# Scaling an attention layer's output instead of its probabilities, with the value product in another orientation

## The reference

```python
q = (x @ w_q).reshape(b, n, HEADS, DIM_HEAD).transpose(0, 2, 1, 3)
k = (x @ w_k).reshape(b, n, HEADS, DIM_HEAD).transpose(0, 2, 1, 3)
gates = jax.nn.sigmoid((x @ w_gate).reshape(b, n, HEADS, EXPERTS).transpose(0, 2, 1, 3))
sel = jnp.argmax(gates, axis=-1)
gm = jax.nn.one_hot(sel, EXPERTS, dtype=x.dtype) * gates
values = jnp.einsum('bhne,ehdk,bnd->bhnk', gm, value_experts, x)
sim = jnp.einsum('bhid,bhjd->bhij', q * SCALE, k)
...
attn = jax.nn.softmax(sim, axis=-1)
out = jnp.einsum('bhij,bhjk->bhik', attn, values)
out = jnp.einsum('bhne,ehkd,bhnk->bhnd', gm, output_experts, out)
return out.sum(axis=1)
```

## Time and profile before

| | |
|---|---|
| time, median of 3 runs | 2442.16 us (2441.66 to 2443.49) |
| the profiled execution: time, span | 2442.16 us, 2439.8 us |
| TensorE busy | 2118.5 us (87%) |
| VectorE busy | 1668.6 us (68%) |
| ScalarE busy | 883.3 us (36%) |
| GpSimd busy | 616.6 us (25%) |
| mean granted TensorE clock | 0.922 of full |

### The profile page before, as it was taken

How to read it: one execution, slowest core, us unless ns; L and a number is a source line. 1 busy time by engine, 2 the same in 40 slices (tenths; PEclk the granted TensorE clock), 3 DMA queues, 4 the chain that set the end, 5 groups by cost and what they waited for, 6 DMA issues and landing times. The chain is left out here.

```text
span 2439.8 us, 40010 instructions
## 1 busy us (share of the span) xinstructions
PE 2118.5 (87%) x12915; PEld 1156.1 (47%) x12915; DVE 1668.6 (68%) x3418; ACT 883.3 (36%) x1559; POOL 616.6 (25%) x834
## 2 busy tenths in 40 slices
PE   4659999999999789999999899599979999859865
PEld 2634444444444356666666544255544444325431
DVE  4757776786777567777777599477745656436668
ACT  3522212211220056666666444033322222223335
POOL 4641110111111155555555332322100000021201
PEclk8569999999999899999999999699979999979975
DMA  3403212220321321111111000000000000010001
GB/s 100 147 1 71 54 29 59 59 63 17 70 53 42 100 69 36 36 32 32 35 31 35 14 0 1 5 12 12 10 4 0 0 0 0 0 28 13 12 4 34
DMA packets 116410, 80.38 MB, mean 33 GB/s; under 512 B 92777, under 2 KB 111081, under 8 KB 111812
## 3 DMA queue, kind: packets, MB, share of 16 engines
q1 hardware_dynamic: 116292, 78.91, 13.4%
HBM read 55.08 MB, written 2.82 MB: 24 GB/s over the span
## 5 line engine op out<-in xcount | busy, mean ns | idle before, releaser
L1015 PE MATMUL l0f_acc<-l0f_z,w_all 128*128 128x512 f32 x512 | 233.3, 618 | 22.7 <-DVE l0f_z L1227 22.7
L912 POOL TENSOR_TENSOR l0f_v<-l0f_val,l0f_top 64x256 f32<-64x256 f32 x128 | 78.4, 613 | 504.4 <-DVE l0f_val L1190 496.8
L966 PE MATMUL l0f_work<-w_all,l0f_xs 128*128 128x512 f32 x384 | 183.5, 600 | 9.9 <-DVE l0f_val L1185 8.6
L1015 PEld LDWEIGHTS l0f_acc<-l0f_z,w_all 128*128 128x128 f32 x512 | 100.6, 198 | 154.7 <-issue 127.5
L241 POOL TENSOR_SCALAR var_eps<-mean_var 128x4 f32<-128x4 f32 (+1 forms) x64 | 14.7, 229 | 569.5 <-DVE mean_var L225 567.6
L2263 PE MATMUL a_score<-keys_by_head,a_qT 128*64 128x512 f32 x512 | 144.7, 647 | 10.8 <-DMA keys_by_head<-w_all 10.8
L2765 DVE TENSOR_TENSOR l2f_work<-l2f_work,l2f_pu 128x512 f32<-128x512 f32 x104 | 71.5, 688 | 120.5 <-ACT l2f_work L2676 119.0
L2676 ACT ACTIVATE l2f_work<-l2f_pg 128x512 f32<-128x512 f32 x104 | 62.1, 597 | 206.9 <-PE l2f_pc L2616 206.8
L1190 DVE COPY_PREDICATED l0f_val<-l0f_oh,l0f_work 128x512 f32<-128x512 int32 x160 | 116.6, 729 | 22.7 <-PE l0f_work L966 7.8
L2621 PE MATMUL l2f_acc<-l2f_work,w_all 128*128 128x512 f32 x208 | 107.8, 600 | 11.1 <-DVE l2f_work L2769 11.1
L1685 DVE TENSOR_REDUCE l1x_ms_k<-l1x_sq_k 128x8 f32<-128x512 f32 x64 | 43.9, 686 | 102.9 <-ACT l1x_sq_k L1571 102.7
(11 more groups left out here) (369 smaller groups left out, 4873.7 us busy)
## 6 DMA issues: line engine op xcount, KB each, us to landing
l0f_first_mask<-onehots SPq DMA_DIRECT2D x32, 512.0 KB, 5.7
w_all<-onehots SPq DMA_DIRECT2D x32, 512.0 KB, 11.9
l1x_v<-l1x_vr SPq DMA_DIRECT2D x256, 64.0 KB, 2.1
w_all<-in_weights SPq DMA_DIRECT2D x1, 4640.0 KB, 16.6
l0x_m_b<-running_max SPq DMA_DIRECT2D x16, 256.0 KB, 4.5
keys_by_head<-w_all SPq DMA_DIRECT2D x256, 8.0 KB
keys_by_head<-ctxT_all SPq DMA_DIRECT2D x256, 8.0 KB
w_all<-in_weights SPq DMA_DIRECT2D x1, 2500.5 KB, 8.6
```

The lines of the kernel that those rows point to most:

```text
L912: nc.gpsimd.tensor_tensor(v2[a * SEQ:(a + 1) * SEQ, t % 2, b, :, :], val[r, t % 2, :, :].rearrange("p (c a) k -> p c a k", a=2)[:, :, a, : ...
L966: nc.tensor.matmul(value_banks[e % 3][:, :], xs[:, t * P:(t + 1) * P], ve[:, e, :], start=True, stop=True).then_inc(ve_done, 1)
L1015: nc.tensor.matmul(acc[:, :], oe[:, n % E, n // E, :], z[:, n % Z, :], start=(n == 0), stop=(n == C * E - 1)).then_inc(acc_done, 1)
```

## The change

The probabilities are no longer scaled before the value product. They are transposed as soon as the exponentials are there. The value product is turned round: the transposed probabilities are the weights, and `v2`, now with the two heads of a pair side by side and zeros between (cleared once at the start), is the data, so eight matmuls of 128 rows and 128 columns give the output with tokens on partitions. VectorE scales that output from PSUM into a new buffer `og` (`scale_out`); TensorE transposes `og` back, four transposes a tile (`turn_out`), into the bank `turn`, from which ScalarE makes `oT`. The order of the work around it is changed on TensorE, ScalarE and VectorE.

```diff
--- before.py
+++ after.py
@@ -840,12 +840,13 @@
-        v2 = sb("v2", [P, 2, 2, C, HD])
+        v2 = sb("v2", [P, 2, 2, C, 2, HD])
...
+        og = sb("og", [P, H * HD])
@@ -894,6 +894,7 @@
+                nc.gpsimd.memset(v2[:, :, :, :, :, :], 0.0).then_inc(setup_done, 1)
@@ -910,7 +911,7 @@
-                                v2[a * SEQ:(a + 1) * SEQ, t % 2, b, :, :],
+                                v2[a * SEQ:(a + 1) * SEQ, t % 2, b, :, a, :],
@@ -935,7 +936,7 @@
-                pe.wait_ge(setup_done, count(3))
+                pe.wait_ge(setup_done, count(4))
@@ -967,7 +968,7 @@
                         if e == 2 and between:
                             between()
-                        if e == 5 and later:
+                        if e == 4 and later:
                             later()
@@ -984,8 +985,8 @@
                 def turn_probs(g, t):
                     n = g * G + t
-                    pe.wait_ge(prob_ready, count(n + 1))
-                    pe.wait_ge(pT_ready, count(n))
+                    pe.wait_ge(exp_done, count(n + 1))
+                    pe.wait_ge(oT_ready, count(n))
@@ -995,17 +996,22 @@
                 def values(g, t):
                     n = g * G + t
                     pe.wait_ge(pT_ready, count(n + 1))
-                    pe.wait_ge(oT_ready, count(n))
+                    pe.wait_ge(og_ready, count(n))
                     pe.wait_ge(v2_ready, count(n * 4 + 4))
-                    pe.sem_inc(may_multiply, 1)
                     for c in range(C):
                         for b in range(2):
-                            for a in range(2):
-                                r = slice(a * SEQ, (a + 1) * SEQ)
-                                q = slice(b * SEQ, (b + 1) * SEQ)
-                                ins = nc.tensor.matmul(po[r, c * P + b * SEQ:c * P + (b + 1) * SEQ], v2[r, t % 2, b, c, :],
-                                                       probT[r, c, q], start=True, stop=True)
+                            q = slice(b * SEQ, (b + 1) * SEQ)
+                            ins = nc.tensor.matmul(po[q, c * P:(c + 1) * P], probT[:, c, q],
+                                                   v2[:, t % 2, b, c, :, :].rearrange("p a e -> p (a e)"),
+                                                   start=True, stop=True)
                     ins.then_inc(pv_done, 1)
+
+                def turn_out(g, t):
+                    pe.wait_ge(og_ready, count(g * G + t + 1))
+                    for c in range(C):
+                        ins = nc.tensor.transpose(turn[:, c * P:(c + 1) * P], og[:, c * P:(c + 1) * P],
+                                                  core.const("ident"))
+                    ins.then_inc(o_turned, 1)
@@ -1028,7 +1034,7 @@
                     for t in range(G - 1):
-                        expert_values(g, t + 1, None, lambda: turn_probs(g, t))
+                        expert_values(g, t + 1, (lambda: turn_out(g, t - 1)) if t else None, lambda: turn_probs(g, t))
                         scores(g, t + 1)
                         values(g, t)
@@ -1038,13 +1044,19 @@
                     if more:
                         logits(g + 1)
-                        project(g + 1, range(0, C))
+                        project(g + 1, range(0, 2))
+                    turn_out(g, G - 2)
+                    if more:
+                        project(g + 1, range(2, C))
                     turn_probs(g, G - 1)
                     if more:
                         project(g + 1, range(C, C + 2))
                     values(g, G - 1)
                     if more:
-                        project(g + 1, range(C + 2, 2 * C))
+                        project(g + 1, range(C + 2, C + 3))
+                    turn_out(g, G - 1)
+                    if more:
+                        project(g + 1, range(C + 3, 2 * C))
                     output_experts(g)
@@ -1106,9 +1118,9 @@
                 def copy_oT(g, t):
-                    act.wait_ge(pv_done, count(g * G + t + 1))
+                    act.wait_ge(o_turned, count(g * G + t + 1))
                     act.wait_ge(z_done, count(g * C * E))
-                    nc.scalar.activation(oT[:, :, t * P:(t + 1) * P], po[:, :].rearrange("p (c q) -> p c q", c=C),
+                    nc.scalar.activation(oT[:, :, t * P:(t + 1) * P], turn[:, :].rearrange("p (c q) -> p c q", c=C),
                                          ACT.Copy).then_inc(oT_ready, 1)
@@ -1119,21 +1131,25 @@
                     for t in range(G - 1):
+                        if t:
+                            copy_oT(g, t - 1)
                         copy_pT(g, t)
-                        exp(g, t + 1)
-                        copy_oT(g, t)
                         if t == 0:
                             copy_onehots(g)
+                        exp(g, t + 1)
                         if t == 1 and normed:
                             norm_scalar(core, nc, act, ns, g - 1, misc)
                     if more:
-                        copy_q(g + 1, range(0, C))
+                        copy_q(g + 1, range(0, 2))
+                    copy_oT(g, G - 2)
+                    if more:
+                        copy_q(g + 1, range(2, C))
                     copy_pT(g, G - 1)
                     if more:
-                        copy_k(g + 1, range(0, 2))
+                        copy_k(g + 1, range(0, 3))
                     copy_oT(g, G - 1)
                     if more:
-                        copy_k(g + 1, range(2, C))
+                        copy_k(g + 1, range(3, C))
                         gate_tanh(g + 1)
@@ -1161,7 +1177,6 @@
-                    after(dve, v2_ready, u * G * 4)
@@ -1188,8 +1203,8 @@
-                        if 0 < e <= len(between):
-                            between[e - 1]()
+                        if e == 1 and between:
+                            between()
@@ -1212,11 +1227,14 @@
-                def scale_probs(g, t):
+                def scale_out(g, t):
                     n = g * G + t
                     dve.wait_ge(gated, count(n + 1))
-                    nc.vector.tensor_tensor(prob[:, t % 2, :, :], prob[:, t % 2, :, :], bcast(tot[:, t % 2, 0, :], 2, SEQ),
-                                            ALU.mult).then_inc(prob_ready, 1)
+                    dve.wait_ge(pv_done, count(n + 1))
+                    dve.wait_ge(o_turned, count(n))
+                    nc.vector.tensor_tensor(og[:, :].rearrange("p (h e) -> p h e", h=H),
+                                            po[:, :].rearrange("p (h e) -> p h e", h=H),
+                                            bcast(tot[:, t % 2, 0, :], 2, HD), ALU.mult).then_inc(og_ready, 1)
@@ -1240,10 +1258,12 @@
                     for t in range(G - 1):
                         if t == 1 and normed:
                             norm_apply(core, nc, dve, ns, g - 1)
-                        pick(g, t + 1, (lambda: totals(g, t), lambda: scale_probs(g, t)))
+                        pick(g, t + 1, (lambda: scale_out(g, t - 1)) if t else None)
                         softmax(g, t + 1)
+                        totals(g, t)
+                    scale_out(g, G - 2)
                     totals(g, G - 1)
-                    scale_probs(g, G - 1)
+                    scale_out(g, G - 1)
                     if more:
                         pick_experts(g + 1)
                     masked_outputs(g)
```

More of the change, by code:

```diff
@@ L863, in l0_ffn @@
         score_done, sub_done, exp_done, tot_done = sem("score_done"), sem("sub_done"), sem("exp_done"), sem("tot_done")
-        p_turned, pT_ready, pv_done, prob_ready = sem("p_turned"), sem("pT_ready"), sem("pv_done"), sem("prob_ready")
-        oT_ready, z_done = sem("oT_ready"), sem("z_done")
-        may_multiply = sem("may_multiply")
+        p_turned, pT_ready, pv_done, og_ready = sem("p_turned"), sem("pT_ready"), sem("pv_done"), sem("og_ready")
+        o_turned, oT_ready, z_done = sem("o_turned"), sem("oT_ready"), sem("z_done")
         oh_stored = core.sem("onehots_stored")
@@ L1069, in _ @@
             def _(act):
-                act.wait_ge(setup_done, count(3))
+                act.wait_ge(setup_done, count(4))
                 def copy_q(u, chunks):
@@ L1155, in _ @@
             def _(dve):
-                dve.wait_ge(setup_done, count(3))
+                dve.wait_ge(setup_done, count(4))
                 prio = bcast(core.const("prio"), 1, G * H)
@@ L1176, in pick_experts, with pick @@
                     ch.done()
-                def pick(g, t, between=()):
+                def pick(g, t, between=None):
                     for e in range(E):
```

## The result

The changed kernel takes 2466.41 us (median of 4, 2465.31 to 2469.52) against 2442.17 before: 24.2 us slower, a ratio of 1.0100 with a 95% interval of 1.0083 to 1.0118. The prediction was 2474, slower.

The account below looks back on a forecast made before the run. TensorE was taken to bound the stage (busy 79.12 of 84.98 us a group). Groups and clearing, 15.8 + 2.0 + 4.2 + 1.75 = 23.8 us, plus 8.5 for the clock, on 2442.16 gave 2474 us, range 2454 to 2484.

Parts of the forecast that it names:

- The wait for `og`: TensorE waits mid-value-matmuls for VectorE's scaled output: about 3.0 us once in each of seven groups, 0.8 in other steps.
- Rival (c): TensorE's waits are hidden, only its added instructions count: 12 + 1.75 us, giving 2456 us; chance 0.15.
- Step to tile 1: Tile loop, up to tile 1's score matmul: no transposes of og, no totals and scaling between picks, gain 0.93 us.
- Step to tile 2: Tile loop, tile 1's to tile 2's score matmul: TensorE idles about 3.0 us for og, step costs 2.2 us.
- Step to tile 3: Tile loop, tile 2's to tile 3's score matmul: TensorE waits 0.8 us for og, step costs 0.82 us.
- Boundary: Tile 3's scores to first output expert: choice of experts after last scaling, ScalarE's tanh ending in a tie; 0.54 us longer.
- Sum over groups 1 to 6 without the clock: Groups 1 to 6, each 2.63 us longer from the steps and boundary: 15.8 us.
- Group 0 and the clearing: Stage start: group 0, with no normalization inside, 2.0 us longer; clearing v2 once on the path, 1.75 us.
- Last group: No next group fills its end: scaling, transposes, copy and hand-overs 2.1 us, with tile loop 2.1, 4.2 us longer.
- The clock: Half-clock stretches after the new 3.0 us wait, five of seven groups at 1.7 us: 8.5 us, bounds 0 and 15.3.
- rival (b): The clock falls after every long wait, at the boundaries too: 2466 + 15 = 2481 us; chance 0.15.
- Rival (a): Waits as computed, clock spared in the new ones: 2442.2 + 23.8 = 2466 us; chance 0.22 with times near it.

Follow-up runs that it names:

- e1: Changed kernel with the transposes of og one value matmul later (after e = 3, the probabilities' after e = 5): 2441.18 us, ratio 1.0003.
- e2: Changed kernel with VectorE's scaling of og straight behind the totals, ahead of the normalization and the next picks: 2436.74 us, ratio 0.9990.
- e8: Kernel before with the four transposes of the probabilities done twice in each tile, into the same place: 2456.11 us, ratio 1.0051.
- e9: Changed kernel with the previous group's normalization ahead of tile 0's totals, while GpSimd still forms v2: 2476.42 us, ratio 1.0158.
- e10: Changed kernel with the choice of experts ahead of the last scaling of og, ScalarE's order left alone: 2467.83 us, ratio 1.0123.
- e4: Changed kernel with the choice of experts ahead of the last scaling of og and ScalarE's tanh ahead of the copies of kb: 2446.39 us, ratio 1.0028.
- e7: Changed kernel with v2 cleared behind the copy of xs and not ahead of it: 2468.59 us, ratio 1.0108.
- e3: Changed kernel with eight matmuls, their result overwritten, on TensorE ahead of its long wait for og in the step to tile 2: 2462.21 us, ratio 1.0083.
- e11: e5 with the previous group's four normalizations spread behind picks 3 to 6 of tile 2: 2408.81 us, ratio to the kernel before 0.9877.
- e5: Kernel before with ScalarE's tanh ahead of the copies of kb, and TensorE waiting for those copies: 2413.05 us, ratio 0.9887.
- e6: Changed kernel with the edits of e2, e4 and e7 together: 2418.32 us, ratio to the kernel before 0.9907.
- e12: e6 with the previous group's normalizations spread behind picks 3 to 6 of tile 2: 2411.61 us, ratio to the kernel before 0.9888.

## Why the prediction was right, point by point

- *The wait for `og` is the cause of the loss*: shown, by e1 (wait moved) and e2 (its answer moved). Rival (c), the added transposes alone, falls for the kernel as changed: with them all in place and the waits gone the total is that of before. Their price is real (e8, 1.54 us a group). That about as much comes back in e1 and e2, whose periods are 0.2 and 0.7 us below the one before, is measured; that it comes from the totals moved into VectorE's idle slot is read from the shorter step to tile 1 and not tested alone.
- *Step to tile 1*: gain 0.93 predicted, 11.23 - 10.17 = 1.06 measured.
- *Step to tile 2*: cost 2.2 predicted, 12.56 - 11.22 = 1.34 measured. This is the term that was mis-sized. The walk took the previous group's normalization at 1.91 us, its duration beside GpSimd's `v2`; in the new order GpSimd is done, and it took 1.03. So the wait was 2.10 us and not 3.0. e9 shows it by putting the two together again: 2.7.
- *Step to tile 3*: 0.82 predicted, 0.67 measured (wait 0.8 predicted, 0.68 measured).
- *Boundary*: 0.54 predicted, 0.56 measured (gap 3.2 predicted, 3.06 measured). The tie of the two chains is in the trace, 0.09 us apart, and e10 and e4 agree with it.
- *Sum over groups 1 to 6 without the clock*: 15.8 predicted, 9.1 measured. Six steps to tile 2 at 0.86 too much are 5.2 of the difference.
- *Group 0 and the clearing*: 3.75 predicted, 4.15 measured, the clearing's 1.74 shown in e7's first wait.
- *Last group*: 4.2 predicted, 4.56 measured. The near match is partly luck: some 1.7 us of it are slow clock, and its step to tile 2 cost 1.69 us and not 2.2.
- *The clock*: 8.5 us predicted for five new stretches at the new wait, none more at the boundaries. Up to group 6's first output expert it was seven more, 11.6 us: four at the new wait and three at the boundaries, one of them the second half of the doubled one. That makes neither the forecast's count nor rival (b)'s: (b) had every long wait followed by a stretch, which held at the boundaries but not at the new wait. e3 shows the cause, TensorE's idleness. Rival (a), the clock spared, gives by chance the measured total (2466), but its mechanism didn't hold.
- *The total*: the direction, the mechanism and the range held, and the total was 8 us too high. Some 5.7 us too much for the seven steps to tile 2 were made good in part by 3 us too little for the clock. Another 2.7 us lie in the blocks around the stage, which were shorter in the profile of the changed kernel. The forecast period of 88 to 89 us came out (88.2 in groups with two stretches) from shorter waits and more slow clock than forecast, which is luck.
- *Open*: what decides whether a given wait is followed by a slow stretch. Waits of 2.10 us were in four of six cases in the changed kernel and five of six in e4, with the same work around them. The boundary gap of 3.0 to 3.1 us was in five of seven before and in e1, in three in e2, in all seven in the changed kernel. A change in the tile loop so shifts the clock at boundaries that it does not touch, by some 8 us between e2 and the changed kernel (3 stretches there against 8). Open too are the later blocks' differences of up to 8 us among kernels with the same code there.

## What to carry to other kernels

Where one engine must wait for an answer made between another's pieces of work, walk both queues once in absolute times: an answer placed after piece 1 can't arrive before piece 2's slot is over, and moving the wait by one instruction or the answer ahead of the pieces was worth all 24 us here, about half of them as clock that no longer fell. Look at what the last short instruction of a long queue releases: a 0.23 us tanh, behind eight copies of `kb` and the copy of `oT`, cost 3 us a group on the bounding engine, more than the change under study, and moving it gave 28 us. When a duration is carried into a new order, ask what ran beside it in the old one.

## What the runs showed of the hardware

- VectorE's four 128x128 fp32 normalizations of SBUF data took 1.91 us from start to next start beside GpSimd's two-input multiplications and 1.03 after them; their own length was 1.99 and 1.11 us, and 1.81 in e9, partly beside them. In the kernel before one of them lasts from 443.79 to 444.57 us, while a GpSimd multiplication runs from 443.87 to 444.49; alone one takes 0.33 (e11). The Trainium skill (GPSIMD Engine Reference, Specifications) says that GpSimd shares its SBUF interfaces with VectorE, with contention for VectorE's two-port modes or two SBUF inputs. The trace agrees that VectorE is slowed, with 1.81 against 1.11 in e9; that these normalizations, with one tensor as input, run in a two-port mode is not shown. GpSimd's own four multiplications took 2.68 to 2.69 us either way.
- How often a wait of TensorE was followed by a stretch at half clock, at 1.7 us each (for the boundary in groups 0 to 6; for the new wait in groups 1 to 7, as group 0 has no long one):

| wait of TensorE | where | followed |
|---|---|---|
| 0.26 us | boundary in e5, e11 | 0 of 7 each |
| 0.4 us (filled) | new wait in e3 | 0 of 7 |
| 1.5 to 1.6 us | boundary in e4, e6, e12 | 0 of 7 each |
| 1.8 us | new wait in the last group of e4, e10 | 0 of 1 each |
| 2.1 us | new wait in the changed kernel, e4, e7, e10 | 4, 5, 4, 3 of 6 |
| 2.21 us | new wait in the last group of the changed kernel, e7 | 0 of 1 each |
| 2.5 to 2.7 us | new wait in e9 | 7 of 7 |
| 3.0 to 3.1 us | boundary before, in e1, e2, e3, e8 | 5, 5, 3, 5, 5 of 7 |
| 3.0 to 3.1 us | boundary in the changed kernel, e7, e9, e10 | 7 of 7 each |

- An instruction that doesn't depend on the one before it was free between two dependent picks: with a 0.33 us normalization between them their distance stayed at 0.86 us (e11).
